# Graph attention and graph convolution in one kernel: attention probabilities turned by transposing DMA transfers instead of TensorE transposes

## The reference, cut to what matters

```python
# x is 1024x512, adj is a 1024x1024 mask made from 16384 edges
h = relu(layernorm(x))
q, k, v = h @ Wq + bq, h @ Wk + bk, h @ Wv + bv
a = q @ k.T / sqrt(512)
a = a * adj + (1 - adj) * NEG
x = x + softmax(a) @ v
h = relu(layernorm(x))
h = agg(h @ W1 + b1)          # agg: sums over edges, weighted by 1/sqrt(degree)
h = relu(batchnorm(h))
x = x + agg(h @ W2 + b2)
```

## Time and profile before

| | |
|---|---|
| median of 3 runs | 340.11 us (339.83 to 340.81) |
| profiled execution, its own time | 340.02 us |
| span in the profile | 338.2 us |
| PE, PEld busy | 320.2 us, 247.5 us |
| DVE, ACT, POOL busy | 200.9 us, 112.9 us, 54.6 us |
| granted TensorE clock | 1.0 of full speed |

### The profile page before, as it was taken

One profiled execution on the slowest core, in us unless ns is written; L12 is line 12 of the kernel. 1 busy time (PEld: TensorE's weight loads), 2 busy tenths in 40 slices (PEclk: granted clock), 3 DMA queues, 4 the chain that ended last, 5 costly groups with the idle time before them and its releaser, 6 DMA issues.

```text
span 338.2 us, 4827 instructions
## 1 busy us (share of the span) xinstructions
PE 320.2 (95%) x1466; PEld 247.5 (73%) x1466; DVE 200.9 (59%) x456; ACT 112.9 (33%) x183; POOL 54.6 (16%) x96
## 2 busy tenths in 40 slices
PE   1898889999999999899999999999999999999996
PEld 0776456777666687788888888888778887887884
DVE  5889999986869514346263636446541257559221
ACT  1909123443464412422342322232621205514000
POOL 5113000000000081512306150120101014300000
PEclk9999999999999999999999999999999999999999
DMA  7912100000230060140202030000000000000041
GB/s 217 320 39 64 62 0 1 3 0 23 102 125 0 2 124 0 36 151 1 64 1 62 2 93 0 2 0 0 0 3 0 0 2 1 2 0 0 28 150 73
DMA packets 17477, 14.83 MB, mean 44 GB/s; under 512 B 11184, under 2 KB 11440, under 8 KB 17456
## 3 DMA queue, kind: packets, MB, share of 16 engines
q1 hardware_dynamic: 17456, 14.56, 14.4%
HBM read 10.36 MB, written 2.10 MB: 37 GB/s over the span
## 4 chain that ended last, share of the span: by engine, by line
PE 78%; DVE 10%; ACT 5%; issue 3%; DVEq 1%; POOL 1%; DMA 1%; SPq 0%; ACTq 0%; POOLq 0%
PE ps L787 17%; PE ps L789 16%; PE ps L788 16%; PE ps L1065 9%; PE ps L850 8%; PE ps L984 5%; PE ps L868 3%; PE ps L927 2%; DVE src_oh L606 2%; PE ps L816 1%; ACT cnt L458 1%; PE ps L948 1%; DMA edge_i<-src_in 1%; DVE bnst L756 1%; DVE g L753 1%
## 5 line engine op out<-in xcount | busy, mean ns | idle before, releaser
L606 DVE TENSOR_SCALAR src_oh<-iota,ecol 128x512 f16 x172 | 48.9, 349 | 1.7 <-PE ps L850 0.9
L850 PE MATMUL ps<-src_oh,dst_oh 128*128 x172 | 41.2, 381 | 2.0 <-DVE dst_oh L608 2.0
L389 ACT ACTIVATE cnt<-ps 64x512 int16<-64x512 f32 x32 | 18.9, 591 | 37.8 <-PE ps L855 37.4
L850 PEld LDWEIGHTS ps<-src_oh,dst_oh 128*128 x172 | 18.3, 114 | 17.8 <-issue 5.5
L984 PE MATMUL ps<-cnt,qh 128*128 128x512 f32 x128 | 30.1, 391 | 0.2 <-ACT cnt L458 0.2
L1065 PE MATMUL ps<-qh,cnt 128*128 128x512 f32 x128 | 29.3, 390 | 0.0
L984 PEld LDWEIGHTS ps<-cnt,qh 128*128 128x128 f32 x128 | 23.9, 188 | 5.5 <-issue 0.6
L1065 PEld LDWEIGHTS ps<-qh,cnt 128*128 128x128 f32 x128 | 23.9, 188 | 5.2 <-DVE vb L768 0.3
L787 PE MATMUL ps<-v,pT 128*128 128x512 f32 x64 | 25.0, 391 | 1.0 <-DVE pT L667 1.0
L787 PE MATMUL ps<-kT,qh 128*128 128x512 f32 x64 | 25.4, 397 | 0.0
L686 DVE TENSOR_TENSOR hnT<-ps,hnT 128x512 fp32r<-128x512 f32 x8 | 5.5, 692 | 33.2 <-ACT hnT L450 33.2
(11 more groups left out here) (150 smaller groups left out, 614.0 us busy)
## 6 DMA issues: line engine op xcount, KB each, us to landing
xt<-x_in SPq DMA_DIRECT2D x16, 256.0 KB, 3.1
out<-xt SPq DMA_DIRECT2D x8, 256.0 KB, 2.0
wA_raw<-L_gnn_Wk_in SPq DMA_DIRECT2D x2, 512.0 KB, 6.6
wB_raw<-L_gnn_Wv_in SPq DMA_DIRECT2D x2, 512.0 KB, 8.1
wA_raw<-L_gnn_Wq_in SPq DMA_DIRECT2D x2, 512.0 KB, 3.7
wB_raw<-L_gnn_W_in SPq DMA_DIRECT2D x2, 512.0 KB, 3.8
w_raw<-L_gnn_W_in SPq DMA_DIRECT2D x2, 512.0 KB, 3.8
bias_row<-L_gnn_b_in SPq DMA_DIRECT2D x2, 256.0 KB, 3.7
```

Source lines behind the costliest of these rows:

```text
L389: act.activation(cnt16[rows, a * KC:(a + 1) * KC, w // 2, :], ps[a * WIN:(a + 1) * WIN, i % 2, :].rearrange("p (s n) -> p s n", n=P), ACT. ...
L606: dve.tensor_scalar(src_oh[:, bass.ds(slot, 1), j, :].rearrange("p a n -> p (a n)"), iota[:, :], ecol[:, bass.ds(c + j, 1)], None, ALU.is_ ...
L850: m = pe.matmul(ps[:, i % 2, :], dst_oh[:, bass.ds(slot, 1), :, j].rearrange("p a n -> p (a n)"), src_oh[:, bass.ds(slot, 1), j, :].rearra ...
```

## The change

After exp, ACT writes the probabilities times 32768 as fp16 into `p16[:, 0]`, and DVE writes what fp16 left over into `p16[:, 1]`. Two transposing DMA transfers of 128x1024 fp16 each, on SP's queue, put them into `p16T`. Then ACT and DVE divide the two planes by 32768 as they widen them to the fp32r parts `pT`. The eight PE transposes of each block are gone, and with them the use of banks 4 and 5; `weighted_v` now writes bank 4.

```diff
-ADJ = 4
+ADJ = 2
+P_UNIT = 32768.0
...
+    p16T = sb("p16T", [P, 2, NT, P], F16)
...
+        def turn_p(t, part, split, done, landed):
+
+            sp.wait_ge(S[split], t + 1)
+            if t >= 1:
+                sp.wait_ge(S[done], t)
+            sp.dma_start_transpose(p16T[:, part, :, :], p16[:, part, :]).then_inc(S[landed], 16)
+
         for t in range(ADJ):
             turn_counts(t)
-        sp.wait_ge(S["item_ps"], len(items))
-        load_w(4)
-        for t in range(XT, NT):
-            load_x(NT + t)
-            if t >= 4:
-                turn_counts(t)
+        for t in range(NT):
+            turn_p(t, 0, "p16_hi", "p_hi", "p16_hi_in")
+            turn_p(t, 1, "p16_lo", "p_lo", "p16_lo_in")
+            if t == 0:
+                sp.wait_ge(S["item_ps"], len(items))
+                load_w(4)
+            if t + ADJ < NT:
+                turn_counts(t + ADJ)
+            if XT <= t + 3 < NT:
+                load_x(NT + t + 3)
...
+        def p16_hi(t):
+
+            act.wait_ge(S["exp_done"], t + 1)
+            if t >= 1:
+                act.wait_ge(S["p16_hi_in"], 16 * t)
+            act.activation(p16[:, 0, :], T[:, t % 2, :], ACT.Copy, scale=P_UNIT).then_inc(S["p16_hi"], 1)
+
         def p_hi(t):
-            act.wait_ge(S["pT_ps"], t + 1)
+
+            act.wait_ge(S["p16_hi_in"], 16 * (t + 1))
             if t >= 2:
                 act.wait_ge(S["pv_ps"], t - 1)
...
+            act.activation(pT[:, t % 2, 0, :, :], p16T[:, 0, :, :], ACT.Copy, scale=1.0 / P_UNIT).then_inc(S["p_hi"], 1)
...
-        def p_lo(t):
-            dve.wait_ge(S["p_hi"], t + 1)
...
+        def p16_lo(t):
+
+            dve.wait_ge(S["p16_hi"], t + 1)
+            if t >= 1:
+                dve.wait_ge(S["p16_lo_in"], 16 * t)
+            dve.scalar_tensor_tensor(out=p16[:, 1, :], in0=T[:, t % 2, :], scalar=P_UNIT, in1=p16[:, 0, :], op0=ALU.mult,
+                                     op1=ALU.subtract).then_inc(S["p16_lo"], 1)
             dve.wait_ge(S["exp_done"], t + 1)
             dve.reciprocal(smx[:, 3, t:t + 1], smx[:, 2, t:t + 1]).then_inc(S["rinv_ready"], 1)
+
+        def p_lo(t):
+
+            dve.wait_ge(S["p16_lo_in"], 16 * (t + 1))
+            if t >= 2:
+                dve.wait_ge(S["pv_ps"], t - 1)
+            dve.tensor_scalar(pT[:, t % 2, 1, :, :], p16T[:, 1, :, :], 1.0 / P_UNIT, None, ALU.mult).then_inc(S["p_lo"], 1)
...
-        def p_turn(t):
-            pe.wait_ge(S["exp_done"], t + 1)
...
         def weighted_v(t):
+            pe.wait_ge(S["p_hi"], t + 1)
             pe.wait_ge(S["p_lo"], t + 1)
...
-            if i >= 1:
-                p_turn(i - 1)
```

More of the change, by code:

```diff
@@ L101, in gnn_kernel @@
     hold("region_vb", 4)
-    dst_oh = sb("dst_oh", [P, RING, P, UNROLL], BF16)
+    p16T = sb("p16T", [P, 2, NT, P], F16)
+    dst_oh, p16 = shared([("dst_oh", [P, RING, P, UNROLL], BF16)], [("p16", [P, 2, N], F16)])
+    hold("region_dst_oh", 4)
     ecol = sb("ecol", [P, NCH + UNROLL], F32)
@@ L148, in gnn_kernel @@
     deg_ready degm_ready degm_ps flag_ready dinv_ready
-    s_ps mask_set masked top_ready exp_done rinv_ready pT_ps p_hi p_lo pv_ps xb_ready x1_ready
+    s_ps mask_set masked top_ready exp_done rinv_ready p16_hi p16_lo p16_hi_in p16_lo_in p_hi p_lo pv_ps xb_ready x1_ready
     bn_ready ln2_coef h2_ready h2T_ps h2T_hi h2T_lo w1_ps h1_tmp h1_hi h1_lo
@@ L330, in mask_fill @@
             if t >= 2:
-                pool.wait_ge(S["pT_ps"], t - 1)
+                pool.wait_ge(S["p16_lo"], t - 1)
             pool.memset(T[:, t % 2, :], NEG / SCALE).then_inc(S["mask_set"], 1)
@@ L461, in _ @@
         for i in range(NT + 2):
+            if 2 <= i <= NT:
+                p_hi(i - 1)
             if i >= 2:
@@ L464, in _ @@
                 h2T_hi(i - 2)
+            if i < NT:
+                softmax_exp(i)
+            if i == 1:
+                act.wait_ge(S["hT_half_used"], 1)
+                p_hi(0)
+            if i < NT:
+                p16_hi(i)
+            if i == 0:
+                hi_of(("q", 1, 1))
+                split_w(3)
             if i == 1:
                 hi_of(("q", 1, 2))
[L467 to L470, removed]
                 hi_of(("q", 1, 3))
[L472 to L477, removed]
             if i == NT + 1:
@@ L676, in residual @@
             dve.wait_ge(S["pv_ps"], t + 1)
-            dve.scalar_tensor_tensor(out=x1[:, t, :], in0=bank(6), scalar=smx[:, 3, t:t + 1], in1=xt[:, n % XT, :],
+            dve.scalar_tensor_tensor(out=x1[:, t, :], in0=bank(4), scalar=smx[:, 3, t:t + 1], in1=xt[:, n % XT, :],
                                      op0=ALU.mult, op1=ALU.add).then_inc(S["x1_ready"], 1)
@@ L686, in h2T_lo, with h1_tmp, h1_lo @@
             dve.tensor_tensor(hnT[:, 1, :], bank(7), hnT[:, 0, :].bitcast(F32), ALU.subtract).then_inc(S["h2T_lo"], 1)
-        def h1_out(t):
+        def h1_tmp(t):
             dve.wait_ge(S["w1_ps"], t + 1)
             dve.tensor_tensor(vb[:, t % 2, :], bank(7), bias_row[:, 1, :], ALU.add).then_inc(S["h1_tmp"], 1)
+        def h1_lo(t):
             dve.wait_ge(S["h1_hi"], t + 1)
@@ L698, in _ @@
         for i in range(NT + 2):
+            if 2 <= i <= NT:
+                p_lo(i - 1)
             if i >= 2:
                 h2T_lo(i - 2)
[L701 to L709, removed]
             if i < NT:
@@ L712, in _ @@
                 add_loops(i)
-            if i >= 2:
-                h1_out(i - 2)
+            if i == 0:
+                large_flag()
+            if i == 1:
+                dve.wait_ge(S["hT_half_used"], 1)
+                p_lo(0)
+            if i >= 2:
+                h1_tmp(i - 2)
+            if i < NT:
+                p16_lo(i)
+            if i == 0:
+                lo_of(("q", 1, 1))
+            if i == 1:
+                lo_of(("q", 1, 2))
+                lo_of(("q", 1, 3))
+            if i >= 2:
+                h1_lo(i - 2)
             if i == NT - 1:
@@ L918, in scores @@
             m.then_inc(S["s_ps"], 1)
-        def p_turn(t):
-            pe.wait_ge(S["exp_done"], t + 1)
[L922 to L929, removed]
         def weighted_v(t):
+            pe.wait_ge(S["p_hi"], t + 1)
             pe.wait_ge(S["p_lo"], t + 1)
-            if t == 0:
-                pe.wait_ge(S["item_lo"], nth(("q", 1, 2)))
             if t >= 1:
@@ L937, in weighted_v @@
             for k in range(NT):
-                m = three(bank(6), lambda a: pT[:, t % 2, a, k, :], lambda a: v[:, k, a, :], k == 0, k == NT - 1)
+                m = three(bank(4), lambda a: pT[:, t % 2, a, k, :], lambda a: v[:, k, a, :], k == 0, k == NT - 1)
             m.then_inc(S["pv_ps"], 1)
@@ L1012, in _ @@
         h2_turn(NT - 2)
-        p_turn(NT - 1)
         times_w1(NT - 2)
```

4 lines of the change are left out of this document (removed).

## The result

The changed kernel takes **335.62 us** (median of 4 runs, 335.29 to 336.16) beside 339.97 (339.82 to 340.81) for the kernel before: ratio 0.9868, 95% interval 0.9847 to 0.9889. It is faster by 1.3%, 4.4 us where 3.5 was forecast. The profiled execution took 335.55 us with a span of 333.7.

The account below looks back on a forecast made before the run. PE, busy 95% of the span, was taken as the bound. Gains of 3.1 us at the start and 0.4 behind the loop, 0 in the loop, took 340.02 to 336.5 us; range 335.6 to 338.8, the forecast's own 335.8 to 337.6.

Parts of the forecast that it names:

- Transposes in the loop: Middle iterations: removing PE's transposes (0.94 us each) gains 0, since they fill a wait for the W1 product's input.
- the chain of 2.08 us stays: Iterations 2 to 7: layer norm's transposes to W1 product still take 2.08 us, so the iteration stays 15.19 us.
- The start: Before the first product with v: PE's waits and transposes go, so it starts at about 139.45, gaining 3.1 us.
- Behind the loop: First sparse sum after the loop: count conversions end earlier, the sum runs through without a wait, gaining 0.4 us.
- 3.1 + 0.4: Sum of the gains at the start and behind the loop, 3.5 us off the profiled 340.02.
- The lock of POOL: Layer norm's coefficients in the loop: `p_lo` may make POOL 0.5 us late, 0.6 spare; cost 0 to 0.1 per iteration.
- Block 1's planes behind the W2 load: Block 1's transfers, queued behind 1 MB of W2, land at about 147.0 and 148.4; cost 0, up to 0.8 once.
- The rival of late transfers: Six loop iterations: planes landing late delay PE through ACT; 348.5 us if landing takes 8 us; chance 7%, 5 slower.
- the forecast's rule: A high plane landing over 6.0 us after issue delays PE by the rest, in each of six iterations.

Follow-up runs that it names:

- e5: Kernel before, with PE turning only one of the eight pieces of the probabilities in blocks 1 to 6; 339.79 us, ratio 0.9991.
- e2: Changed kernel with one more, long met wait on DVE ahead of `h2T_lo`'s own wait; 336.40 us, ratio 0.9889 to the kernel before.
- e3: Changed kernel with block 0's mask and exp back in their old place; 340.24 us, ratio 1.0002 to the kernel before.
- e4: Kernel before, with only block 0's mask and exp moved up as in the change; 338.89 us, ratio 0.9966.
- e1: Changed kernel, product with v ahead of the W1 product in iterations 2 to 6, DVE's residual ahead of `h1_tmp` there; 340.79 us.
- e8: Changed kernel with DVE's widening of the low plane (`p_lo`) done twice; 338.63 us, ratio 0.9954 to the kernel before.
- e11: Changed kernel with eight one-element DVE writes between the loop and the sums; 335.89 us, ratio 0.9879 to the kernel before.
- e7: Changed kernel with an extra transposing transfer of the high plane that must land before the two planes are sent; 349.60 us.
- e6: e1 with ACT's split of W2 ahead of `h1_hi`; 333.17 us, ratio 0.9783 to the kernel before.

## Why the prediction came out as it did

- *Transposes in the loop, gain 0.* The mechanism was right: a wait of 0.71 stands in their place, and e5 shows it on the kernel before. (0.94 was named. The chain is 0.07 shorter, and 0.16 is the last score matmul's own end, which the view counts as busy.) **The first step that failed is "the chain of 2.08 us stays", and with it "Gain: 0".** It overlooked that `p_lo`, moved in between, parts `h2T_lo` from a second wait on DVE. The chain is 2.01, worth 0.36 in the loop and 0.07 once behind it. e2 put the 0.07 back.
- *The start, 3.1.* Measured 3.19. The first product with v began at 139.39 where 139.45 was forecast, and both widenings at 138.23 where 138.3 was. e3 and e4 show that the gain needs both halves.
- *Behind the loop, 0.4.* Measured 0.44 for the sum that runs through, and the chain's 0.07 again.
- **The second step that failed: the sum "3.1 + 0.4" has no term for the W2 stage.** 0.44 us came there from DVE's fourth sum, which starts without the old delay. The row with 0.61 stood in the trace of before, and the forecast did not read that far. Its going away was luck: by the table above it depends on how many instructions stand ahead, and five to eight more bring one back (e1, e2, e8, e11).
- *The range.* Against the forecast 0.09 (start) + 0.36 + 0.07 (chain) + 0.04 (sum) + 0.04 (up to the W2 stage) + 0.44 = 1.04 us more was gained up to the second sparse sum, all one way. The range allowed 0.9 on that side, since every open cost had been counted as a loss and no open gain was looked for.
- *The lock of POOL, "0 to 0.1 per iteration".* The lock came, 0.50 us as worked out, and cost PE nothing: 0.13 us were left. The Trainium skill (SBUF — State Buffer, section "SBUF: two separate sides") says that whichever of the two engines starts first keeps the shared port for its whole instruction; the rows at 177.19 and 177.25 us agree, and the forecast had left open whether the widening counts among the instructions that do so.
- *Block 1's planes behind the W2 load.* Forecast for 147.0 and 148.4. ACT and DVE started on them as they landed:

```profile
147.11 1.06 ACT L458 ACTIVATE pT<-p16T 128x1024 fp32r<-128x1024 f16 x1 [5.72 <-DMA p16T<-p]
148.54 0.69 DVE L703 TENSOR_SCALAR pT<-p16T 128x1024 fp32r<-128x1024 f16 x1 [1.64 <-DMA p16T<-p]
```

The layer norm behind ACT's row starts at 148.23 (forecast 148.2), and it cost nothing, as forecast.

- *The rival of late transfers* did not occur: the planes landed 3.2 us after issue in the median. Its price was put too low in two ways. The room of 2.7 us (2.1 on ACT and 0.6 on PE) was taken from one iteration for all. ACT's widening of block 2 ends at 162.28, the layer norm wants ACT at 163.72, and PE has 0.28 to spare, 1.7 us; reckoned alike the room is 0.7 for block 1, 2.4 for block 3 and 3.0 from block 4 on (191.24 to 194.12, and 0.13). And the path from SP's queue through the x block to the next mask has no term in it. For the 6.3 to 6.4 us of e7's high planes the forecast's rule gives 0.3 to 0.4 us in each iteration; e7 measured waits of 1.3 to 3.2.

## What to carry to other kernels

Before counting an instruction on the bounding engine as a gain, look at what the next instruction there would wait for without it. If a wait stands behind it, the gain is to be had only by putting other work into it, and then every engine's queue has to be walked through once: e1 lost 5 us to one split that stood ahead of a small instruction, and e6 got 7.6 back with a swap. A long wait of PE's can cost a second time, by its clock: it did so for five of the seven waits of 2.0 us and more in the attention loops of e1, e3 and e7.

## What was not expected of the hardware

- A second wait, long met, ahead of a DVE instruction costs 0.07 us where that instruction lies on the path (0.10 instead of 0.03 behind ACT's end; e2, and the last block of the changed kernel).
- DVE showed a delay of 0.37 to 0.39 us at one instruction behind a branch, at a place that its number of instructions alone sets (fourteen traces), with an 8 KB packet of the queue "q14 instruction" 0.6 us behind it. That its instructions load late there is an inference.
- PE's granted clock was 0.76, 0.70 and 0.81 in the 7 to 9 us behind waits of 3.06, 4.11 and 2.61 us (e3, e1). In e7 it was 0.60 and then 0.77 in the 5.8 us behind 3.19, and 0.62 for 4.45 us behind 2.14 and 0.72, but 1.00 behind 1.32, 2.04 and 2.26. The waits of 0.71 in each iteration and of 1.41 behind the loop left the changed kernel at 0.998 over its span.
- DVE's widening from 16 bit with a single SBUF input holds POOL off for its whole 0.69 us (e8, and the changed kernel at 177.19).
